# Mamba-style layer behind attention and experts: the depthwise convolution as shifted products on TensorE, its taps folded into the projection's weights, its bias as a bf16 product

## The reference, cut to what matters

```python
xz = jnp.einsum('btd,ed->bte', x, W_in)
x_inner, z = (xz[..., :D_INNER], xz[..., D_INNER:])
xc = jnp.transpose(x_inner, (0, 2, 1))
xc = jax.lax.conv_general_dilated(xc, conv_w, window_strides=(1,), padding=[(D_CONV - 1, 0)], feature_group_count=D_INNER, dimension_numbers=('NCH', 'OIH', 'NCH')) + conv_b[None, :, None]
x_conv = jnp.transpose(silu(xc), (0, 2, 1))
...
dt = jax.nn.softplus(jnp.einsum('btr,dr->btd', dt_low, W_dt) + b_dt)
...
_, h = jax.lax.associative_scan(comb, (dA, dBx), axis=1)
```

## Time and profile before

| | before |
|---|---|
| median of 3 runs | 2718.4 us |
| lowest and highest | 2712.68 and 2719.95 us |
| the profiled execution | 2723.16 us |
| its span, first to last instruction | 2721.4 us |
| its mean granted TensorE clock | 0.915 |

### The profile page before, as it was taken

The page is one execution under the profiler, slowest core; times in us unless marked ns, Lnnn a source line. Parts: engine busy times, 40 slices in busy tenths (PEclk is TensorE's granted clock), DMA queues, the critical chain, the costliest instruction groups (busy, mean ns, idle before and its releaser), DMA issues.

```text
span 2721.4 us, 41804 instructions
## 1 busy us (share of the span) xinstructions
PE 2139.4 (79%) x11705; PEld 1002.0 (37%) x11840; DVE 1956.9 (72%) x3193; ACT 1624.3 (60%) x4159; POOL 1724.0 (63%) x2236
## 2 busy tenths in 40 slices
PE   4778988879798887878788887978888797877543
PEld 3344433434344333434343433434334343332110
DVE  2444658787786868777686868778587877778776
ACT  2655656666575666666566665757666566644442
POOL 1012258586776858577685857678585867777643
PEclk9889999999899999989899998989999899999665
DMA  7535395766667586665768676666857667454442
GB/s 141 90 61 102 58 177 109 148 129 143 122 112 156 104 158 127 147 125 117 136 120 166 121 133 126 127 130 124 164 109 146 127 140 129 97 127 128 118 117 69
DMA packets 534880, 338.84 MB, mean 125 GB/s; under 512 B 353929, under 2 KB 453177, under 8 KB 534201
## 3 DMA queue, kind: packets, MB, share of 16 engines
q1 hardware_dynamic: 534652, 336.16, 62.3%
HBM read 242.21 MB, written 26.74 MB: 99 GB/s over the span
## 4 chain that ended last, share of the span: by engine, by line
PE 30%; DVE 22%; POOL 16%; issue 14%; DMA 7%; ACT 7%; SPq 4%; POOLq 0%; ACTq 0%; DVEq 0%
DVE work L1241 6%; DMA bc<-bc_rows 5%; PE bank L623 5%; POOL work L1235 4%; POOL work L1248 4%; PE bank L909 3%; PE bank L954 3%; PE bank L651 3%; DVE nmax L631 3%; PE bank L1271 3%; POOL zh L967 2%; PE bank L972 2%; DVE step L1046 2%; PE bank L1072 2%; ACT probs L641 2%
## 5 line engine op out<-in xcount | busy, mean ns | idle before, releaser
L1235 POOL TENSOR_TENSOR work<-work,bc 128x512 f32<-128x512 f32 x512 | 658.5, 1292 | 188.7 <-PE bank L1271 132.7
L1241 DVE TENSOR_TENSOR_SCAN work<-bank,work 128x512 f32<-128x512 f32 x512 | 622.0, 1215 | 170.7 <-POOL work L1235 111.4
L1248 POOL TENSOR_TENSOR work<-work,bc 128x512 f32<-128x512 f32 x436 | 559.8, 1287 | 147.3 <-DVE work L1241 132.4
L967 POOL TENSOR_TENSOR zh<-zh,w_bc 128x512 f32<-128x512 f32 x256 | 326.9, 1277 | 403.4 <-DVE zh L960 403.1
L1224 ACT ACTIVATE bank<-work,neg_a 128x510 f32<-128x510 f32 x512 | 353.5, 691 | 370.1 <-DVE work L1241 349.5
L641 ACT ACTIVATE probs<-bank,nmax 128x256 f32<-128x256 f32 x1024 | 477.2, 479 | 69.2 <-DVE nmax L631 68.2
L631 DVE TENSOR_REDUCE nmax<-bank 128x2 f32<-128x512 f32 x512 | 336.0, 676 | 196.1 <-PE bank L623 195.9
L954 PE MATMUL bank<-h_b,w_t 128*128 128x512 f32 x512 | 293.7, 657 | 113.3 <-ACT probs L641 105.3
L651 PEld LDWEIGHTS bank<-ident,probs 128*128 128x128 f32 x2048 | 268.3, 151 | 293.8 <-issue 249.3
L659 ACT ACTIVATE probs_t<-bank 128x512 f32<-128x512 f32 x512 | 305.1, 596 | 106.6 <-PE bank L681 72.6
L623 PE MATMUL bank<-ke,q_all 64*64 64x256 f32 x4096 | 302.4, 413 | 84.4 <-DVE zh L960 47.8
(11 more groups left out here) (194 smaller groups left out, 2545.6 us busy)
## 6 DMA issues: line engine op xcount, KB each, us to landing
work<-dt_rows SPq DMA_DIRECT2D x256, 512.0 KB, 5.8
ke<-low SPq DMA_DIRECT2D x256, 256.0 KB, 5.8
w_bc<-w_rows_d SPq DMA_DIRECT2D x256, 256.0 KB, 5.1
q_all<-q_rows SPq DMA_DIRECT2D x1024, 8.0 KB
bc<-bc_rows SPq DMA_DIRECT2D x64, 256.0 KB, 8.4
x_in<-in_x SPq DMA_DIRECT2D x32, 256.0 KB, 5.5
dt_rows<-step SPq DMA_DIRECT2D x16, 512.0 KB, 3.5
dt_rows<-step SPq DMA_DIRECT2D x32, 256.0 KB, 2.5
```

Of the source, the lines that this page charges most:

```text
L967: nc.gpsimd.tensor_tensor(zh[:, n % 3, :], zh[:, n % 3, :], w_bc[:, n % WB, :], ALU.mult).then_inc(m_p, 1)
L1235: nc.gpsimd.tensor_tensor(hb[at % HB], ring[n % RING][:, 1, :], bc[:, s, :], ALU.mult).then_inc(s_dbx, 1)
L1241: nc.vector.tensor_tensor_scan(hb[at % HB], decay_bank(p, m)[:, :], hb[at % HB], 0.0, ALU.mult, ALU.add).then_inc(s_h, 1)
L1248: nc.gpsimd.tensor_tensor(hb[at % HB], hb[at % HB], bc[:, SG + batch(m)[2], :], ALU.mult).then_inc(s_hc, 1)
```

## The change

The convolution leaves DVE. A filter of four taps behind a projection is four projections with scaled weights, each shifted in time. So `s_in_x_tensor` becomes five products into bank 4: one bf16 product for the bias (`b1_w` times `ones`, with 256 more columns in `b1_w`), and four fp32 products with `w_conv`, the last three of which read `h_s` shifted and write 510, 508 and 506 columns. `s_conv_vector` goes, and so does `conv_s`: tanh and silu read bank 4. Bank 4 is therefore free for the next gate only once silu is done, and the gate waits for `s_xc`. Tanh and silu move to steps 349 and 359. `w_conv` is made once: eight diagonal matrices on ACT at step 110 of the first pair, eight products on PE at step 118, and two copies on ACT at step 122. The first softplus gets the wait on `dt_out[1]` that the first convolution had.

```diff
             m_end_scalar=324, s_norm_scalar=337, s_turned_scalar=344, s_conv_scalar=[349, 359],
...
-            s_conv_vector=[[348, 352, 352, 352], [359, 360, 360, 360]], s_silu_vector=[357, 364],
...
+            s_silu_vector=[349, 359], s_zgate_vector=[392, 399], f_res_vector=512,
...
-                    pe.wait_ge(s_cv, KC * (2 * ((n - GAP["x"][h]) // NE) + h + 1))
+                    pe.wait_ge(s_xc, 2 * ((n - GAP["x"][h]) // NE) + h + 1)
...
             if h:
-                pe.wait_ge(s_cv, KC * (2 * p + 1))
-            nc.tensor.matmul(bank[4][:, :], win_t[:, h * P:(h + 1) * P], h_s[:, :], start=True, stop=True).then_inc(s_xz, 1)
+                pe.wait_ge(s_xc, 2 * p + 1)
+            x, y = segments(h_s[:, :]), segments(bank[4][:, :])
+            nc.tensor.matmul(bank[4][:, :], b1_w[:, NE * P + h * P:NE * P + (h + 1) * P], ones[:, :], start=True, stop=False)
+            for back in range(KC):
+                lo = (h * KC + KC - 1 - back) * P
+                last = nc.tensor.matmul(y[:, :, back:], w_conv[:, lo:lo + P], x[:, :, 0:T - back], start=False, stop=(back == KC - 1))
+            last.then_inc(s_xz, 1)
...
-        def s_conv_vector(dve, p, h, back):
...
         def s_conv_scalar(act, p, h):
-            act.wait_ge(s_cv, KC * (2 * p + h + 1))
+            act.wait_ge(s_xz, 4 * p + h + 1)
...
-            nc.scalar.activation(conv_t, conv_s, ACT.Tanh).then_inc(s_ct, 1)
+            nc.scalar.activation(conv_t, bank[4][:, :], ACT.Tanh).then_inc(s_ct, 1)
...
-            nc.vector.scalar_tensor_tensor(x_conv(p, h), conv_t, 1.0, conv_s, ALU.add, ALU.mult).then_inc(s_xc, 1)
+            nc.vector.scalar_tensor_tensor(x_conv(p, h), conv_t, 1.0, bank[4][:, :], ALU.add, ALU.mult).then_inc(s_xc, 1)
...
+        def conv_diag_scalar(act):
+            act.wait_ge(s_setv, 1)
+            for k in range(NH * KC):
+                last = nc.scalar.activation(conv_d[:, k * P:(k + 1) * P], ident[:, :], ACT.Copy, scale=conv_w[:, k // KC, k % KC:k % KC + 1])
+            last.then_inc(s_cdiag, 1)
+
+        def conv_weights_tensor(pe):
+            pe.wait_ge(s_cdiag, 1)
+            pe.wait_ge(s_set, 1)
+            for k in range(NH * KC):
+                last = nc.tensor.matmul(bank[4 + k // KC][:, k % KC * P:(k % KC + 1) * P], win_x[:, k // KC * D:(k // KC + 1) * D],
+                                        conv_d[:, k * P:(k + 1) * P], start=True, stop=True)
+            last.then_inc(s_cprod, 1)
```

More of the change, by code:

```diff
@@ L43 @@
 BPARTS = 3
+BROW = NE * P + 2 * P
 DI, NH, NS, DTR, KC = 256, 2, 16, 8, 4
@@ L240, in build @@
         b_y, b_back, b_x = sem("b_y"), sem("b_back"), sem("b_x")
-        s_xz, s_z, s_zg, s_cv, s_ct, s_xc, s_bc, s_bcc = (
-            sem("s_" + n) for n in ("xz", "z", "zg", "cv", "ct", "xc", "bc", "bcc"))
+        s_xz, s_z, s_zg, s_ct, s_xc, s_bc, s_bcc = (
+            sem("s_" + n) for n in ("xz", "z", "zg", "ct", "xc", "bc", "bcc"))
+        b1_conv, s_cdiag, s_cprod, s_cw = (sem(n) for n in ("b1_conv", "s_cdiag", "s_cprod", "s_cw"))
         s_dtp, s_dt, s_dtx_p, s_z0, s_z1, s_c, s_hd = (
@@ L1631, in step_vector @@
             for h in range(NH):
-                for k in range(KC):
-                    p = due("s_conv_vector", st, h, k)
-                    if p is not None:
-                        s_conv_vector(dve, p, h, k)
-            for h in range(NH):
                 p = due("s_silu_vector", st, h)
@@ L1740, in setup_vector, with conv_weights_scalar @@
             nc.vector.tensor_scalar(neg_a[:, :], neg_a[:, :], -1.0, None, ALU.mult).then_inc(s_setv, 1)
+        def conv_diag_scalar(act):
[10 more added lines that the diff above has]
+            last.then_inc(s_cprod, 1)
+        def conv_weights_scalar(act):
+            act.wait_ge(s_cprod, 1)
+            for h in range(NH):
+                last = nc.scalar.activation(w_conv[:, h * KC * P:(h + 1) * KC * P], bank[4 + h][:, :], ACT.Copy)
+            last.then_inc(s_cw, 1)
+        CONV_AT = 118
         B1_AT = [24 + 8 * k for k in range(10)]
```

92 lines of the change are left out of this document (45 added, 47 removed).

## The result

The changed kernel takes 2735.6 us (median of 5 runs), beside 2717.8 us for the kernel before: a ratio of 1.0074, 95% interval 1.0053 to 1.0094, so it is 0.7% or 18 us slower. The profiled execution took 2732.7 us, with a span of 2730.9 us.

A forecast was written before the change was run, and what follows sets the result against it. No engine as such bounds the kernel, but PE's ordered work sets the middle pairs' stretch before the step product. Terms of 12 x 3.6 + 5.2 + 2 + 2 + 3 + 2.5 = 57.9 us on 2718.4 gave 2776 us, range 2750 to 2800.

The forecast's parts named there:

- What bounds: No engine as such; in pairs 1 to 12 PE's own ordered work, 18.68 of 20.91 us up to the step product.
- the walk: Instruction-by-instruction tracing of a middle pair's stretch with the added products: gates never wait for silu, step product 3.6 us later.
- first pair: Stretch of 17.79 us with no scan beside it and hardly any PE idle time: 5.2 us longer.
- pair 13: Stretch of 24.06 us including a 2.37 us wait for the taps: between 0 and 3.6 us longer, taken as 2.
- pairs 14 and 15: Experts without attention, 2 us of loss; then the last pair at granted clock 0.60, DVE waiting for silu, 3 us.
- the sum: Whole kernel: 12 x 3.6 + 5.2 + 2 + 2 + 3 + 2.5 = 57.9 us on the median; chance 0.68.
- PE has room: Rival: half of the 3.6 us delay is made up behind the step product, 2754 us; chance 0.13.
- sign of error: Stated check: step product late by 3.6 us but next scan not late would mean the slack lies in the DMAs.
- The start: Making w_conv once: scaled copies, products and two copies, 0 to 6.8 us on the path, taken as 2.5.
- The middle pairs: Pairs 1 to 12: 5.57 us of added products less vanished waits delays each step product 3.6 us.
- Waits on top: Rival: ACT's and DVE's standstill behind tanh and silu reaches PE, 24 us more, 2800 us; chance 0.12.
- DVE was the bound: Rival: added products as cheap as bf16 ones, so vanished waits and DVE's relief win, 2700 us; chance 0.03.

The follow-up runs named there:

- the idle products: Kernel before plus two fp32 products of 512 columns ahead of each x projection, results overwritten: 2752.6 us; with 32 bytes of padding 2747.6, with 480 bytes 2729.1.
- few queries: Changed kernel, with the transfers of q_all<-q_rows moving one sixteenth of their rows from the second pair on: 2744.8 us, runs of 2727 to 2754 us.

## Why the prediction was wrong

*What bounds, and the walk.* Right. The stretch from the first bias product to the step product was given as 24.3 to 24.8 us, and is 24.45; the gates wait for nothing; ACT waits 2.4 and 3.5 us for PE and DVE 3.5 us for ACT, where 3 to 4 were given. The price of a shifted product (0.86 us, no surcharge for the offset) holds. In the first pair the stretch grew by 5.55 us (5.2 given). In pair 13 the idle time of the stretch swallowed all of it and more: with the bias product the stretch is 23.47 us instead of 24.06, where 2 us of loss were given. From its step product to the end of the span the execution took 356.2 us instead of 349.9, 6.3 more; 5 were given for pairs 14 and 15. A pair before was given as 157.0 us, the length of the window that was read the earlier trace rows; the mean of pairs 1 to 12 is 156.3.

*What was left out.* The step that failed is the sum. It had a term for every instruction that was added, removed or moved, and none for the tiles that move in memory with them. At equal places the change costs 44 us (2760.3 against 2716.3 us, 32 bytes past), 47 us (2756.5 against 2709.7 us, a multiple of 64) or 39 us (2735.6 against 2696.3 us, multiples of 256). The result of 18 us is that cost less the 20 to 25 us that the new places give: padding to multiples of 256 takes 20 and 22 us off the kernel before, and leaving them adds 21 and 25 us to the changed one. The prediction looked at the transfers of this stretch only as something that might absorb a delay, the rival that PE has room. Its time of 2754 us was nearer than the forecast, but half of the delay does not come back: of the 45 us by which the idle products lengthened the stretches, 35, 38 and 33 us reached the end at the three kinds of place. So that rival is right by a sixth to a quarter of the delay, not by half. I named as a sign of error that the next scan is not late, "then the slack lies in the DMAs". The sign came; the cause in brackets was wrong.

*What was too large.* At equal places 39 to 47 us remain of 57.9. The start was put at 2.5 us and cost nothing that can be seen: the first projection begins at 320.1 us, beside 326.1 before, and between 320.0 and 326.8 us in the other kernels without the new start. Pair 13 is named above. The middle pairs were put at 12 x 3.6 us, and their stretches did grow by 3.55. But the stretches of all pairs together grew by 55 us, and 39 to 47 us reached the end. The idle products lost as large a share of their 45 us on the way (33 to 38 reached the end) with all the taps still on DVE, so DVE's relief is not needed to explain it, and no run shows that it is worth more than PE's waits.

What goes with it in all kernels is TensorE's granted clock, the other term that the sum put at nothing. Its mean over all executions, for the three kinds of place (32 bytes past, a multiple of 64, a multiple of 256), is 0.915, 0.915 and 0.918 without the change, 0.919, 0.919 and 0.924 with the idle products, and 0.924, 0.923 and 0.929 with the change. The place of the tiles moves it, and so does more work on PE. Two rows of busy time show it, from the step product of pair 1 to that of pair 13, before and after:

```profile
495.91:2371.50 1875.59, 1557.48 (x8729) 734.55 (x8836) 1425.30 (x2296) 1201.99 (x3100) 1354.74 (x1712) 0.94 0.68 132
```

```profile
493.11:2374.73 1881.62, 1594.71 (x8884) 758.00 (x9003) 1349.05 (x2199) 1202.36 (x3100) 1359.06 (x1712) 0.96 0.62 131
```

That is 18 us a pair at the lower level of 1.2 GHz before and 12 us after (16 us in the changed kernel with 32 bytes of padding), nearly all of it 30 to 90 us behind the step product. In the first 10 us of these, where the next scan waits for its rows, PE is busy for 5.5 us before and for 6.6 us after. Between executions of one and the same kernel a mean clock higher by 0.01 goes with about 14 us less (with few queries in the changed kernel, 2727 us at 0.937 and 2754 us at 0.923). By this estimate the 0.007 to 0.011 that the change adds at equal places would be 10 to 15 us, about the 8 to 16 us that are missing, and 5 to 8 us of what the places give would come by way of the clock. No run held the clock fixed, so this is not shown.

*The other rivals.* Waits on top did not come. That DVE was the bound would have decided at 0.30 us for each added product; with bf16 products of 0.22 us the kernel did become faster than before, by 1.2%, and at equal places by 12 to 14 us (2682.3 against 2694.4 and 2696.3 us). With fp32 products the added work on PE costs more than all that leaves DVE gives back.

## What to carry to other kernels

When a change adds or drops a tile, even of 8 bytes, compare the addresses of the tiles that transfers write before and after, and time both versions at the same remainder of 256 bytes; else the price of the edit is mixed with that of its place. A queue that moves the same bytes in a smaller share of time, in the same stretch beside the same work, is the sign to look for. And a convolution as shifted fp32 products is a bad trade on a TensorE that already sets the pace: each product cost 0.5 to 0.7 us of its 0.86, while of what it replaces on DVE only TensorE's waits for it, 1.63 us a pair here, were seen on the path.

## What the runs showed of the hardware

- Transfers into SBUF tiles at multiples of 256 bytes ran at 258 to 267 GB/s with all DMA engines full; 64 bytes past such a multiple it was 247 to 251, and 32 bytes past a multiple of 64 it was 233 to 244. Over the kernel this is worth 0.7 to 0.9%. Each packet goes by the place of its own target: to a tile 32 bytes past a multiple of 64 one of 1024 bytes took 82 to 90 ns instead of 69 to 75, one of 4096 bytes 269 to 279 ns instead of 254 to 264.
- TensorE read bf16 operands with a stride of two 16-bit words (the upper halves of fp32 numbers), weights and moving data, at the rate of packed ones: 0.22 us for 506 to 510 columns.
- An fp32 product that writes two runs of 253 to 255 columns at an offset took as long as one of 512 in one run (586 to 620 ns a record, beside 621).
- TensorE's mean granted clock rose with its own work and with faster transfers, 0.915 to 0.929, and executions of one kernel were the faster the higher it was (0.923 to 0.937, 2754 to 2727 us).
